# A two-layer graph attention kernel: x and the adjacency go out first on two queues, and layer 0's row work is moved and respread

## What is computed

```
h = maximum(layernorm(x), 0)
x = x + elu(softmax(where(adj > 0, leaky_relu(s1[:, None] + s2[None, :]), -9e15)) @ (h @ W))      # layer 0; s1 = h W a1, s2 = h W a2
h = maximum(layernorm(x), 0)
x = x + elu(softmax(where(adj > 0, q @ k.T / sqrt(128), -9e15)) @ v)                              # layer 1; q, k, v = h W.T + b
```

## Time and profile before

| | us |
|---|---|
| median of 3 runs (1713.73 to 1715.44) | 1714.29 |
| the profiled execution | 1712.56 |
| its span, first to last instruction | 1710.8 |
| busy: PE / VectorE / ScalarE / GpSimd | 1176.5 / 1308.5 / 875.0 / 1136.8 |
| bytes moved by DMA | 372.37 MB |

### The profile page before, as it was taken

How to read it: one execution, slowest core, us unless ns; L and a number is a source line. 1 busy time by engine, 2 the same in 40 slices (tenths; PEclk the granted TensorE clock), 3 DMA queues, 4 the chain that set the end, 5 groups by cost and what they waited for, 6 DMA issues and landing times.

```text
span 1710.8 us, 22463 instructions
## 1 busy us (share of the span) xinstructions
PE 1176.5 (69%) x5362; PEld 916.9 (54%) x5362; DVE 1308.5 (76%) x6020; ACT 875.0 (51%) x1763; POOL 1136.8 (66%) x1206
## 2 busy tenths in 40 slices
PE   2657785776766687777765467777777777767776
PEld 1334453554544454554455456666666666656664
DVE  3578996998888898888897476777767777777766
ACT  2768776878777777777652232332333223332322
POOL 1237775766666766666666477777777777777773
PEclk9888877787778777777765566656656665665565
DMA  9879999999999999999922122222222222222221
GB/s 291 348 262 390 394 395 400 393 398 374 368 387 375 391 385 383 382 384 381 385 71 62 49 59 56 65 65 65 63 64 65 65 63 64 65 65 64 64 65 39
DMA packets 122258, 372.37 MB, mean 218 GB/s; under 512 B 34577, under 2 KB 67858, under 8 KB 89362
## 3 DMA queue, kind: packets, MB, share of 16 engines
q1 hardware_dynamic: 75458, 289.83, 44.1%
q0 software_dynamic: 38464, 81.08, 17.1%
q10 hardware_dynamic: 8208, 0.03, 0.3%
HBM read 358.12 MB, written 12.72 MB: 217 GB/s over the span
## 4 chain that ended last, share of the span: by engine, by line
POOL 34%; DVE 19%; DMA 15%; issue 13%; PE 10%; ACT 6%; SPq 2%; POOLq 0%; ACTq 0%; DVEq 0%
POOL arena L609 32%; DMA table<-arena 13%; ACT arena L1187 4%; PE psum L1446 4%; PE psum L1432 3%; POOL arena L579 2%; DMA arena<-in_adj_dram 1%; DVE arena L765 1%; DVE arena L798 1%; DVE arena L880 1%; PE psum L1418 1%; DVE arena L873 1%; DVE arena L768 1%; PE psum L1385 1%; DVE arena L889 1%
## 5 line engine op out<-in xcount | busy, mean ns | idle before, releaser
L579 POOL DMA_INDIRECT arena<-table,arena x576 | 554.3, 962 | 267.2 <-issue 159.5
L609 POOL DMA_INDIRECT arena<-table,arena x576 | 554.2, 962 | 183.9 <-issue 174.9
L1187 ACT ACTIVATE arena<-arena 128x2048 bf16<-128x2048 int32 x256 | 484.9, 1895 | 34.4 <-DMA arena<-in_adj_dram 33.2
L1385 PE MATMUL psum<-arena 128*128 128x512 bf16 x1024 | 293.2, 435 | 23.1 <-ACT arena L1187 22.8
L1418 PE MATMUL psum<-arena 128*128 128x18 f32 x768 | 140.2, 314 | 235.8 <-DVE arena L846 235.5
L880 DVE SCALAR_TENSOR_TENSOR arena<-arena 128x131 f32<-128x131 f32 (+1 forms) x768 | 269.7, 351 | 15.3
L1432 PE MATMUL psum<-arena 128*128 128x131 f32 (+1 forms) x768 | 200.7, 433 | 104.0 <-ACT arena L1320 102.3
L1418 PEld LDWEIGHTS psum<-arena 128*128 128x128 f32 x768 | 126.7, 245 | 268.0 <-DVE arena L846 268.0
L1432 PEld LDWEIGHTS psum<-arena 128*128 128x128 f32 x768 | 179.6, 330 | 107.7 <-issue 107.7
L1385 PEld LDWEIGHTS psum<-arena 128*128 128x128 bf16 x1024 | 114.1, 118 | 161.1 <-issue 73.4
L1129 DVE TENSOR_TENSOR arena<-arena 128x258 f32<-128x258 f32 (+1 forms) x256 | 84.1, 390 | 148.1 <-DMA arena<-table,arena 148.1
(11 more groups left out here) (203 smaller groups left out, 1981.0 us busy)
## 6 DMA issues: line engine op xcount, KB each, us to landing
arena<-in_adj_dram SPq DMA_DIRECT2D x256, 1024.0 KB, 15.9
arena<-table,arena POOLq DMA_INDIRECT x1152
table<-arena POOLq DMA_DIRECT2D x32, 132.0 KB, 5.0
arena<-table SPq DMA_DIRECT2D x64, 66.0 KB, 15.5
table<-arena SPq DMA_DIRECT2D x16, 256.0 KB, 15.3
arena<-table SPq DMA_DIRECT2D x64, 64.0 KB, 1.9
out_dram<-arena SPq DMA_DIRECT2D x16, 256.0 KB, 2.6
arena<-in_x_dram SPq DMA_DIRECT2D x4, 0.5 KB, 12.2
```

The lines of the kernel that those rows point to most:

```text
L579: pool.indirect_dma_start(Gt[:, v % GROUP, c + 1, :], None, table0, bass.IndirectOffsetOnAxis(idx_now[:, v % GROUP, c:c + 1], 0))\
L609: pool.indirect_dma_start(Gt[:, t % GROUP, c + 1, 0:D], None, table1, bass.IndirectOffsetOnAxis(idx_now[:, t % GROUP, c:c + 1], 0))\
L1187: nc.scalar.activation(mask[:, k, q * QUARTER:(q + 1) * QUARTER], adj_sb[:, k, q, :], ACT.Relu, accum_out=sum_all[:, bass.ds(tile, 1), q:q ...
L1385: nc.tensor.matmul(V[k], shifted[:, s, :], mask[:, k, s * 512:(s + 1) * 512], start=(s == 0), stop=False)
```

## The change

- SyncE issues x chunks 0 and 1 and then the adjacency. ScalarE's queue issues the four weights, the four columns, the row of `bv`, x chunks 2 and 3 and then the diagonal.
- VectorE builds its constants first, takes the statistics chunk by chunk, and finishes mean and deviation in two halves. `hide_diag(0, 0)` comes after the statistics of all four chunks.
- `start_rows` moves to GpSimd (two `tensor_scalar` without the ReLU, through a buffer of four units, three units ahead of the writes); `keep_turned` moves from VectorE to ScalarE, as one activation with the ReLU.
- The 32 units go two to a quarter, at quarters n = 3 to 18. TensorE's transposes for quarter n stand behind its pack of that quarter, and ahead of them the projections of the two units before. ScalarE's two `keep_turned` stand behind its read of that quarter.
- `wh_rows` is six units deep instead of four. The transposes use PSUM banks 6 and 3.

```diff
-            for k in range(4):
+            for k in range(2):
                 sp.dma_start(X[:, 16 * k:16 * k + 16, :], x_tiles[:, 16 * k:16 * k + 16, :]).then_inc(x_in[k], 16)
...
-            for n, w in enumerate((W, Wq, Wk, Wv)):
-                sp.dma_start(weights[:, n, :], w).then_inc(consts_in, 16)
...
+        def units_of(n):
+            return range(2 * (n - 3), 2 * (n - 3) + 2) if 3 <= n < 3 + UNITS // 2 else ()
```

GpSimd:

```diff
+            def start_rows(i):
+                pool.wait_ge(shift0_done, 1 + 2 * i // HALF)
+                at_least(pool, h_turned, i - 3)
+                for n in range(2):
+                    m = 2 * i + n
+                    nc.gpsimd.tensor_scalar(h_rows[:, i % 4, n, :], X[:, m, :], rstd[:, m:m + 1], shift[:, m:m + 1],
+                                            ALU.mult, ALU.add).then_inc(h_done, 1)
+            AHEAD = 3
+            for i in range(UNITS + AHEAD):
+                if i < UNITS:
+                    start_rows(i)
+                if i >= AHEAD:
+                    j = i - AHEAD
+                    pool.wait_ge(wh_kept, j + 1)
+                    pool.dma_start(table0[1 + 2 * P * j:1 + 2 * P * (j + 1), :].rearrange("(t p) d -> p t d", p=P),
+                                   wh_rows[:, j % WRITES, :, :]).then_inc(table0_in[j % WRITES], 16)
```

VectorE, opening:

```diff
+            look_at(0)
             dve.wait_ge(consts_in, 16 * 9)
...
+            look_at(1)
+            moments0(0)
...
+            polish0(0)
...
+            look_at(2)
+            look_at(3)
+            moments0(1)
+            dve.wait_ge(diag_in, 16)
...
+            hide_diag(0, 0)
+            polish0(1)
```

VectorE, pass t:

```diff
+                    def keep_units(slot):
+                        if t < UNITS // 8:
+                            for i in range(8 * t + 2 * slot, 8 * t + 2 * slot + 2):
+                                keep_rows(i)
```

ScalarE:

```diff
+            for k in range(2, 4):
+                act.dma_start(X[:, 16 * k:16 * k + 16, :], x_tiles[:, 16 * k:16 * k + 16, :]).then_inc(x_in[k], 16)
             act.dma_start(diag[:, :], flat[0:N * N:N + 1].rearrange("(t p) -> p t", p=P),
...
+            def keep_turned(i):
+                act.wait_ge(h_turned, i + 1)
+                at_least(act, wh_done, i - 1)
+                nc.scalar.activation(hT[:, i % 2, :], turned_ps[i % 2], ACT.Relu).then_inc(hT_done, 1)
...
+            read_quarter(0, 0, 0, 1)
+            root0(0)
+            for q in range(1, QUARTERS):
                 read_quarter(0, 0, q, 1)
+            for i in units_of(3):
+                keep_turned(i)
             read_quarter(1, 1, 0, 1)
+            root0(1)
+            for i in units_of(4):
+                keep_turned(i)
...
                             read_quarter(m, m % 2, q, m // 2 + 1)
+                        for i in units_of(QUARTERS * m + q):
+                            keep_turned(i)
```

TensorE:

```diff
+            def work_on_units(n):
+                for i in units_of(n - 1):
+                    project_rows(i)
+                for i in units_of(n):
+                    turn_rows(i)
...
-                        pack(t + 1, (b + 1) % 2, range(0, 8))
+                        for q in range(2):
+                            pack(t + 1, (b + 1) % 2, range(4 * q, 4 * q + 4))
+                            work_on_units(QUARTERS * (t + 1) + q)
```

More of the change, by code:

```diff
@@ L287, in two_layer_graph_attention @@
         s1_kept = sem("s1_kept")
-        table0_in = [sem(f"table0_in{k}") for k in range(4)]
+        table0_in = [sem(f"table0_in{k}") for k in range(WRITES)]
         adj_in = [[sem(f"adj_in{k}{q}") for q in range(QUARTERS)] for k in range(2)]
@@ L412, in two_layer_graph_attention @@
         UNITS = T // 2
+        HALF = T // 2
+        turned_ps = [bank(6 - 3 * k)[:, 0:2 * P] for k in range(2)]
+        table0_writes = [16 * len(range(k, UNITS, WRITES)) for k in range(WRITES)]
+        def units_of(n):
+            return range(2 * (n - 3), 2 * (n - 3) + 2) if 3 <= n < 3 + UNITS // 2 else ()
         def live(t, lag):
@@ L479, in load_group @@
                         sp.wait_ge(zeros_in, 32)
-                        for k in range(4):
-                            sp.wait_ge(table0_in[k], 16 * UNITS // 4)
+                        for k in range(WRITES):
+                            sp.wait_ge(table0_in[k], table0_writes[k])
                         load_self(0, 0)
@@ L564, in _ @@
             pool.dma_start(table1[0:1, :], zeros[:, 0:D]).then_inc(zeros_in, 16)
[L566 to L571, removed]
+            def start_rows(i):
[14 more added lines that the diff above has]
+                                   wh_rows[:, j % WRITES, :, :]).then_inc(table0_in[j % WRITES], 16)
+            for k in range(WRITES):
+                pool.wait_ge(table0_in[k], table0_writes[k])
             pool.wait_ge(zeros_in, 32)
@@ new lines, in _, with look_at @@
+            nc.vector.tensor_scalar(part_c[:, :], part_c[:, :], (PLACE - 1) / 2 + 1 - 512 * (127 + 6), None, ALU.add)\
+              .then_inc(dve_consts, 1)
+            for k in range(GROUP):
+                nc.vector.tensor_copy(dealt[:, k, 0:P], ident[:, :]).then_inc(dve_consts, 1)
+            DVE_CONSTS = 9 + SEGS
+            def look_at(k):
+                dve.wait_ge(x_in[k], 16)
+                for n in range(16 * k, 16 * k + 16):
+                    nc.vector.bn_stats(stats0[:, n, :], X[:, n, :]).then_inc(stats0_done, 1)
@@ L633, in _ @@
                   .then_inc(dve_consts, 1)
[L634 to L640, removed]
-                nc.vector.tensor_scalar(off_diag[:, k, :], ident16[:, :], neg_diag[:, bass.ds(tile, 1)], None, ALU.mult)\
-                  .then_inc(off_done, 1)
[L644 to L648, removed]
+            polish0(0)
             dve.wait_ge(mixed, 1)
@@ L966, in survey @@
                         total(w, w % 2, D + 3)
-                    if t < 3:
-                        for i in range(12 * t, min(12 * t + 12, UNITS)):
-                            keep_turned(i)
-                            if i:
-                                keep_rows(i - 1)
-                        if t == 2:
-                            keep_rows(UNITS - 1)
+                    keep_units(1)
                     if live(t, 1):
@@ L1244, in survey @@
                     quarter(3)
-                    if t < 3:
-                        for i in range(12 * t, min(12 * t + 12, UNITS)):
-                            start_rows(i)
                     if b == 3 and 0 <= g - 2 < G:
@@ L1392, in pack_end @@
                 nc.tensor.matmul(V[k], ones16[0:1, :], place16[0:1, :], start=False, stop=True).then_inc(packed, 1)
-            pack(0, 0, range(SEGS))
-            pack_end(0, 0, 0, 0)
-            pe.wait_ge(mixed_sb, 12)
             def turn_rows(i):
@@ L1401, in turn_rows @@
                 for n in range(2):
-                    last = nc.tensor.transpose(bank(2 + i % 2)[:, n * P:(n + 1) * P],
-                                               h_rows[:, i % 2, n, :], ident[:, :])
+                    last = nc.tensor.transpose(turned_ps[i % 2][:, n * P:(n + 1) * P], h_rows[:, i % 4, n, :], ident[:, :])
                 last.then_inc(h_turned, 1)
@@ L1412, in project_rows @@
                 last.then_inc(wh_done, 1)
+            def work_on_units(n):
[3 more added lines that the diff above has]
+                    turn_rows(i)
+            pe.wait_ge(dve_consts, 9 + SEGS)
+            pack(0, 0, range(SEGS))
+            pack_end(0, 0, 0, 0)
+            pe.wait_ge(mixed_sb, 12)
+            work_on_units(3)
             def scatter(tt, k, r):
```

134 lines of the change are left out of this document (66 added, 68 removed).

## The result

| | before | changed |
|---|---|---|
| median, range (5 runs each) | 1715.44 (1713.73 to 1716.55) | 1742.09 (1740.54 to 1748.09) |
| the profiled execution, its span | 1712.56, 1710.8 | 1743.03, 1741.0 |

The ratio is 1.0163, 95% interval [1.0152, 1.0174]: the change makes the kernel 1.6% slower, some 27 us. The direction was predicted, the size was not (1723, 1706 to 1742). The two chips on which e5 to e12 ran moved the survey's bytes at 336 to 341 GB/s from 200 to 400 us, where the others moved 385 to 394, and the kernel before timed 2025 and 2040 us there instead of 1714. Up to some 125 us their rates agree with the others' (407 GB/s from 65 to 125 us in e6 as in e14), so their traces are used up to there, and four of the kernels were timed again on another chip (e13 to e16).

A forecast was written before the change was run, and what follows sets the result against it. DMA time lost before 125 us (15.6 us) was taken as the bound, quarter 19 carrying the end: 40 + 79.5 + 2.6 + 9 = 131.1, less 121.6, plus 1: about 10 us later, 1723 us, range 1706 to 1742.

The forecast's parts named there:

- The measure, quarter 19: Start of ScalarE's read of quarter 19, 121.58 us before, expected at 125 to 135; the end moves with it.
- Step 1: The opening, up to the read of quarter 4: about 40 us, 9 us earlier than before.
- the diagonal comes late: Rival, opening: diagonal starved packet by packet beside adjacency loads, quarter 4 at 59, time 1733 to 1743 us; chance 0.17.
- Step 2: Quarters 4 to 18: ScalarE and TensorE take turns instead of overlapping, 5.3 us a quarter, 15 turns, 79.5 us.
- it works as laid out: Rival, whole change: units hide, loads are never short, the 15.6 us come back, 1698 to 1702 us; chance 0.15.
- Step 3: TensorE's clock in the turns: 28% of the time at the lower level adds 9 us, bounds nothing and 31.
- Step 4: The first gather: starts some 12 us behind quarter 19 instead of 5.0, charged 1 us, bounds 0 and 7.
- the sign by which step 4 was to be wrong: Quarter 39 late in a way that the DMA share shows.
- Edits at nothing: start_rows on GpSimd (1.3 to 1.9 us a unit, hidden), keep_rows, decode and lists, six units of wh_rows: no cost charged.

The follow-up runs named there:

- e5: The changed kernel with the opening's queues as before (SyncE: x, weights, adjacency; ScalarE: the diagonal alone), on a disturbed chip: ratio 1.0115.
- e12: e6 with VectorE taking all four chunks' statistics and the first half of moments before waiting for the weights, on a disturbed chip: ratio 0.9705.
- e6: The changed kernel with the opening's queues as before and keep_turned behind the next quarter's read, on a disturbed chip: ratio 0.9894.
- e14: The kernel of e6 timed again on another chip (opening's queues as before, keep_turned behind the next quarter's read): 1691.98 us, ratio 0.9873.
- e13: The kernel of e5 timed again on another chip (changed kernel, opening's queues as before, turns kept): 1730.58 us, ratio 1.0107.
- e16: The kernel before with wh_rows and its semaphores six units deep instead of four, nothing else: 1703.06 us, ratio 0.9933.
- e4: The changed kernel with ten matmuls that nothing reads behind the transposes of each of quarters 4 to 18: 1726.48 us, ratio 1.0074.
- e15: The kernel of e12 timed again on another chip (e14 with all statistics ahead of the wait for the weights): 1690.88 us, ratio 0.9868.
- e2: The changed kernel with keep_turned of each quarter behind ScalarE's read of the next quarter: 1703.88 us, ratio 0.9944.
- e1: The changed kernel with the diagonal's load issued first in ScalarE's queue, ahead of weights and x: 1744.00 us, ratio 1.0178.
- e10: The kernel of e6 once more, on a disturbed chip: ratio 0.978.
- e9: The kernel of e5 once more, on a disturbed chip: ratio 1.0055.

## Why the prediction was wrong in size and right in kind

**The measure, quarter 19.** It was to be read at 125 to 135 us and was read at 148.66. It moved by 27.1 us, quarter 255 by 29.9. In e13 it was 14.8 and 16.6, in e4 12.6 and 14.8, in e16 -8.9 and -10.0: it carries the end within 3 us as long as it is late. Once loads are no longer short it doesn't (e14: -25.7 and -20.9; e15: -31.7 and -22.7).

**Step 1, the opening, is the step that failed.** Quarter 4 was to be read at 40 us and was read at 56.95. The term that failed is the wait for the diagonal: the sum put it at nothing, and it took 16.03 us. The trace of the changed kernel shows it on its own. VectorE had closed the statistics of all four chunks at 37.3 us (34 was the forecast; chunk 3 of x came at 34.07), was ready for the diagonal at 38.09, and stood still until 54.12. From there to quarter 4 are 56.95 - 54.12 = 2.83 us, so without that wait quarter 4 would stand at 40.9, inside the forecast's 37 to 43. This is worked out from one trace; no run moves the diagonal and nothing else. It fits e13, which gave back 12.3 us and not 16, because there VectorE waited 11.92 us for the weights, and its order (e14 against e15: 4.5 us at quarter 5) then counted.

The rival "the diagonal comes late" had all of this: it put the landing at 55 us, quarter 4 at 59 and the time at 1733 to 1743, and the packets alternate 108 to 108 as it said. It got 0.17 because I read SyncE's dry queue in the earlier trace rows as descriptors made in turn, which would have let the diagonal through. No such pause came while loads were to be had. In the kernel before that queue was dry from 12.5 to 13.0 us while its fourth issue of x was still under way (9.69 to 13.96 us); why it was dry no run shows, and as a rule for the adjacency it did not hold.

**Step 2, the turns, held in its mechanism and was some 5 us too long.** 5.3 us at the full clock were forecast; e4's plain turn at a clock of 1.00 is 4.78, and so is the changed kernel's where its clock was high (63.79 to 68.57). With closings the forecast had (79.5 + 2.6 - 0.46) / 15 = 5.44 a turn, and e4 measured 5.13, its first turn at the low clock. The order alone is worth 2.2% (e2 against the changed kernel), and 2.3% with the opening undone (e14 against e13). It is the largest part of what was measured, and the rival "it works as laid out" fell by it.

**Step 3, the clock, held in its mechanism and was 5 us too short.** 9 us were charged and e4 measures 14.4. The price of a low turn was right: 2.1 us more, and the turn of 56.95 to 63.79, wholly at the lower level, took 6.84 against 4.78. The share was wrong: 28% of the time at the lower level was carried over from the lumps, where the clock was 0.86; in the turns it was 0.78, which is 44%, and 0.44 x 2.06 x 15 = 13.6.

So it is partly luck that 79.5 + 2.6 + 9 = 91.1 us were forecast from quarter 4 to 19 and 91.7 came: two errors of about 5 us cancel.

**Step 4, the first gather, was undersized.** It starts 17.4 us behind quarter 19 (166.04), not 12: the last two writes were issued 6.6 us behind it (155.25), and the gather waited 9.20 us for their landing, where 5.0 had been taken. The waits show what hung on it. VectorE waited 9.5 us for gathered rows (line 876), TensorE 12.1 for VectorE (line 870), ScalarE's block copy 11.1 for TensorE (line 1282), and the read of quarter 39 came at 212.67 instead of 173.14. That is 39.5 us late, 12.4 more than quarter 19, with a DMA share of 0.88 from 125 to 200 us: the sign by which step 4 was to be wrong. Most of it was made up by the end of the survey: what quarter 255 loses beyond quarter 19 is 2.9 us, where 1 was charged and 7 was the bound. No run changed the gather alone.

**Edits at nothing.** `start_rows` takes 0.45 us an instruction (3.58 / 8) and 1.63 us a unit with the write's issue, inside the 1.3 to 1.9 that were bounded, and was hidden in the turns. Single instructions took 0.44 to 0.60 us there, beside VectorE's, so no stall of a whole instruction shows. It stopped being hidden when the turns went (e2). Six units of `wh_rows`: VectorE waits for no landed write in the turns, though no run tried four there; in the kernel before they are worth 10.7 us (e16), which I had not looked for, because I asked only what the wait would be after the change.

With quarter 4 at 56.95 in place of 40 the sum is 1723 + 17 = 1740, against 1742 measured: the net error is step 1, step 4 adds 2 us, and the errors of steps 2 and 3 hide each other.

## What to carry to other kernels

When a step is moved between two engines that hand a buffer back and forth, write down the order on both queues: if each waits for the other's step of the *same* round, the times add. Shifting one side by one round was worth 2.2% here, the low clock of the same turns 0.9%. A wait that the sum puts at nothing needs a reason as good as that of any other term. A load of thousands of single elements belongs where its queue has nothing large beside it, and nothing behind it. Count what a stall costs in bytes that were not moved, and take the rate at which they are made up.

## What the runs showed of the hardware that was not expected

- A queue of 4-byte packets beside one of 8 KB packets got exactly one for one (108 to 108, 216 to 216), so 8192 elements took 42.1 us; alone, 2391 packets went in 1 us.
- Behind a load of 8192 elements, the next issues on the same engine's queue stood too: 14.98 us for the first and 2.2 us for each small one up to 29.65 us (e1), 0.45 otherwise. In the changed kernel it was the diagonal's own issue that lasted 10.05 us, behind two loads of x. The table load and the first mask stand behind it.
- In a pattern of work and rest the granted clock went up and down from turn to turn, and ten matmuls a turn that nothing reads brought 0.78 to 0.96 and 15 us (e4).
- Two chips moved the survey at some 339 GB/s (e6: 337 from 200 to 400 us; e14: 385), but at the same 407 from 65 to 125 us; why is not shown. With 3 to 4% of spread in their times, their places up to 125 us were still good to 1.1 us (quarter 19 of e6, e10 and e14: 94.99, 94.84, 95.93). Later ones were not: quarter 19 of e5, e9 and e13 came at 140.89, 142.77 and 136.34.
